# Two tiles per transpose and four half-height silus in a layered sequence kernel on one NeuronCore

## The reference

```python
def body(h, p):
    y = jax.nn.silu(layernorm(h, l1w, l1b))
    y = sconv(y, pr + 1j * pi, lr + 1j * li)     # y[t] = sum over s<=t of p**(t-s) * x[s], real part
    h = h + y * scl
    y = layernorm(h, l2w, l2b)
    y = jax.nn.silu(jnp.einsum('bld,fd->blf', y, w1) + b1_)
    y = jnp.einsum('blf,df->bld', y, w2) + b2_
    return h + y
```

## Time and profile before

| | |
|---|---|
| median of 3 runs | 204.45 us (204.21 to 204.62) |
| the profiled execution, its own time | 204.57 us |
| span of its trace | 202.8 us |
| PE busy | 181.9 us, 90% |
| DVE busy | 157.4 us, 78% |
| ACT busy | 109.8 us, 54% |
| POOL busy | 84.0 us, 41% |
| granted TensorE clock, mean | 0.992 |

### The profile page before, as it was taken

How to read it: one execution, slowest core, us unless ns; L and a number is a source line. 1 busy time by engine, 2 the same in 40 slices (tenths; PEclk the granted TensorE clock), 3 DMA queues, 4 the chain that set the end, 5 groups by cost and what they waited for, 6 DMA issues and landing times.

```text
span 202.8 us, 3759 instructions
## 1 busy us (share of the span) xinstructions
PE 181.9 (90%) x1210; PEld 148.8 (73%) x1210; DVE 157.4 (78%) x547; ACT 109.8 (54%) x281; POOL 84.0 (41%) x142
## 2 busy tenths in 40 slices
PE   0797996859999998999999899999999898988992
PEld 0797995758988788788998689989988444555430
DVE  6898978886588768784977776655899997998872
ACT  1595687524456467637555445462836585863210
POOL 4222269724044422343224522467462735555400
PEclk9999999978999999999999999999999999999999
DMA  5999990000000000000000000000000000002675
GB/s 158 419 376 400 417 368 14 5 0 0 0 5 0 0 3 0 0 3 0 0 0 5 0 0 0 3 0 3 2 0 2 0 3 0 2 0 105 228 283 216
DMA packets 5505, 15.31 MB, mean 75 GB/s; under 512 B 925, under 2 KB 1965, under 8 KB 4462
## 3 DMA queue, kind: packets, MB, share of 16 engines
q1 hardware_dynamic: 5486, 15.07, 19.7%
HBM read 10.87 MB, written 4.19 MB: 74 GB/s over the span
## 4 chain that ended last, share of the span: by engine, by line
PE 68%; DVE 7%; POOL 7%; DMA 6%; ACT 5%; issue 3%; SPq 2%; DVEq 0%; ACTq 0%
PE bank L1508 15%; PE bank L1400 11%; PE bank L1632 7%; PE bank L1490 6%; DMA M<-in_mraw 6%; PE bank L1464 4%; PE bank L1452 4%; POOL RS L360 4%; PE bank L1567 3%; PE bank L1638 3%; POOL M L380 2%; PE bank L1440 2%; PE bank L1556 2%; ACT XA L593 2%; DVE Z L1001 1%
## 5 line engine op out<-in xcount | busy, mean ns | idle before, releaser
L360 POOL TENSOR_TENSOR RS<-SS,nhalf 128x4 f32<-128x4 f32 x36 | 42.9, 1202 | 67.9 <-DVE SS L995 67.6
L1508 PE MATMUL bank<-ffst,HD 128*128 128x128 f32 x256 | 32.7, 283 | 0.0
L1508 PEld LDWEIGHTS bank<-ffst,HD 128*128 128x128 f32 x256 | 31.3, 200 | 0.2
L995 DVE TENSOR_REDUCE SS<-SQ 128x4 f32<-128x260 f32 x36 | 15.2, 421 | 20.9 <-ACT SQ L635 20.3
L1400 PE MATMUL bank<-M,XT 128*128 128x226 f32 x128 | 27.6, 362 | 0.1
L659 ACT ACTIVATE HD<-bank,b1r 128x512 f32<-128x512 f32 x32 | 20.3, 684 | 10.9 <-PE bank L1490 10.8
L1400 PEld LDWEIGHTS bank<-M,XT 128*128 128x128 f32 x128 | 23.2, 189 | 3.6 <-issue 3.1
L635 ACT ACTIVATE SQ<-bank 128x256 f32<-128x256 f32 x36 | 13.8, 383 | 19.6 <-PE bank L1508 9.6
L640 ACT ACTIVATE Y<-bank,cvst 128x512 f32<-128x512 f32 x16 | 12.5, 779 | 15.1 <-PE bank L1452 15.1
L1035 DVE TENSOR_TENSOR_SCAN V<-cvst,U 128x514 f32<-128x514 f32 x16 | 19.5, 1218 | 0.0
L1490 PE MATMUL bank<-Z,w1r 64*128 64x256 f32 x128 | 18.1, 402 | 0.4
(11 more groups left out here) (265 smaller groups left out, 346.0 us busy)
## 6 DMA issues: line engine op xcount, KB each, us to landing
XT<-in_xT SPq DMA_DIRECT2D x4, 1024.0 KB, 11.7
X<-in_x SPq DMA_DIRECT2D x4, 1024.0 KB, 14.0
out<-X SPq DMA_DIRECT2D x8, 512.0 KB, 2.9
w1r<-in_w1d SPq DMA_DIRECT2D x1, 516.0 KB, 16.5
lt<-in_late SPq DMA_DIRECT2D x1, 449.5 KB, 16.3
M<-in_mraw SPq DMA_DIRECT2D x1, 448.0 KB
w2r<-in_w2n SPq DMA_DIRECT2D x1, 256.0 KB, 11.8
winr<-in_win SPq DMA_DIRECT2D x1, 254.0 KB, 2.6
```

Source lines behind the costliest of these rows:

```text
L360: pool.tensor_tensor(RS[:, g, :], SS[:, g, :], nhalf[:, :], ALU.pow).then_inc(done, 1)
L995: dve.tensor_reduce(SS[:, g, :], SQ[:, g, :, :], AX.X, ALU.add).then_inc(done, 1)
L1508: last = pe.matmul(HK[g][:, j * P:(j + 1) * P], HD[:, u % 2, a, at:at + P], ffst[:, L, a * P:(a + 1) * P], start=False, stop=True, skip_gr ...
```

## The change

Units 0 to 3 keep the old transposes and silu. From unit 4 the first half of a unit works in another layout:

- DVE writes the scaled state once (`scale`, 128 x 256) in place of twice (`scale_twice`, 128 x 512). This holds for units 4 to 15, since the first four are written out in `first_steps`.
- `turn1` does two transposes, each of a 128 x 128 block that holds two tiles: the features of tiles 0 and 2 of the group come out on partitions 0 to 63, those of tiles 1 and 3 on partitions 64 to 127, in columns 0 to 255 of bank 0.
- `silu1` is four instructions of 64 partitions x 256 columns: each half of the partitions is read twice and written to the real half and to the imaginary half of `Y`.
- In `setup_late(1)` the product `aux_values @ Wvd.T` is no longer formed by four matmuls; the stored `vpT` is transposed.

```diff
             def silu1(u):
                 g, L = u % GROUPS, u // GROUPS
                 act.wait_ge(t1, u + 1)
-                act.activation(by_seq(Y[:, g, :])[:, :, 1:SL], by_seq(T1B[:, :]), ACT.Silu,
-                               bias=cvst[:, L, LB0:LB0 + 1], scale=cvst[:, L, LW0:LW0 + 1]).then_inc(y1, 1)
+                if u < GROUPS:
+                    act.activation(by_seq(Y[:, g, :])[:, :, 1:SL], by_seq(T1B[:, :]), ACT.Silu,
+                                   bias=cvst[:, L, LB0:LB0 + 1], scale=cvst[:, L, LW0:LW0 + 1]).then_inc(y1, 1)
+                    return
+                for lo in (0, DIM):
+                    for to in (0, DIM):
+                        at = 1 + lo // DIM * P
+                        last = act.activation(by_seq(Y[to:to + DIM, g, :])[:, :, at:at + P],
+                                              by_seq(T1B[lo:lo + DIM, 0:HW]), ACT.Silu,
+                                              bias=cvst[lo:lo + DIM, L, LB0:LB0 + 1],
+                                              scale=cvst[lo:lo + DIM, L, LW0:LW0 + 1])
+                last.then_inc(y1, 1)
...
                 if s < UNITS:
-                    scale_twice(s)
+                    scale(s, rs1, z1)
...
                 if i == 1:
-                    for c in range(VC):
-                        pe.matmul(LB[:, 0:VB], vals[:, c, :], wvd[:, c, :], start=(c == 0), stop=(c == VC - 1))
+                    pe.transpose(LB[:, 0:VB], vpT[:, :], ident[0:VB, 0:VB])
...
-                for j in range(GT):
+                for j in range(2 if GROUPS <= u < UNITS else GT):
```

## The result

The changed kernel takes 214.25 us in the median (213.47 to 215.68, 4 runs) beside 204.33 for the kernel before (4 runs): a ratio of 1.0485 with an interval of 1.045 to 1.052. It is 9.9 us slower where I forecast 1.4 us faster, and lies far outside the range. The profiled execution took 213.60 us, 9.03 more than that of before. Some executions of some kernels here took a few per cent longer than the others of the same kernel; the times are medians of all executions, the ratios compare the others alone.

A forecast was written before the change was run, and what follows sets the result against it. PE, busy 90% and holding 68% of the chain, was taken as the bound, with room on ACT; step terms summed to -1.43 us, giving 203.14 from the profiled 204.57, stated as 203.1 us, eight-in-ten range 201.3 to 205.8.

The forecast's parts named there:

- plain steps: Steps such as 11 to 13: forecast 6.11 us for 6.23; 6.23 or more would show the prediction wrong.
- I take p = 0.465 us per silu: ACT, start to start of half-height silus: 561 ns less 0.10 overlap; four hold ACT 1.86 us where one held 0.68.
- My own slope, 42 us per us of p: ACT from first silu to `z_out`: the change moves by 40 to 42 us per us of time per silu.
- Rival A: ACT, first silu to `z_out`: silus do not overlap, 0.56 us each, sum +2.6, about 207.1 us; chance 0.16.
- `mix_in` and `project` are due earlier than ACT's list reaches them: PE operations between silu and `hidden`: claimed due early enough that their waits have cover; no cost counted.
- the formula 2.75 + 0.25n: ACT's list from silu start to `hidden` after the change, 0.25 us per x copy, against PE's 2.90 us.
- the transposes at 0.11 us each: PE, `turn1`: two fewer transposes give 0.22 us in each of 12 units, 2.6 us if all on the path.
- the state at 0.29: DVE: scaled state falls from 691 to 401 ns, 0.29 us per unit, counting only where PE waits for it.
- the arithmetic of steps 5 to 9: `hidden` to `hidden`, steps 5 to 9: -0.22, -0.74, -0.15, +0.30 and -0.01 us, from PE's and ACT's lists.
- step 8 as a loss: Step 8, where copies keep the silu 3.29 us after `hidden`: 6.32 for 6.02 us, +0.30.
- step 14 at 6.85: Step 14, where the state comes late behind `score_rows`: -0.51 us, from shorter state and transposes.
- the memory product: PE, step 6: a transpose of about 0.11 us replaces 1.08 us, some 0.9 us of PE gone, once.

The follow-up runs named there:

- e12: Changed kernel, all four silus reading and writing only partitions 0 to 63, upper half of Y left out: 207.76 us, ratio 1.018.
- e11: Changed kernel, silus only on partitions 0 to 63 (upper half of Y left out) and x copies in front of silu1: 202.57 us, ratio 0.990.
- e5: Changed kernel with the x copies of a step moved on ACT from behind silu1 to in front of it: 209.60 us, ratio 1.021.
- e9: Changed kernel with silu1 as two silus of 128 partitions x 256 columns, half of Y holding wrong tiles' features: 201.68 us, ratio 0.987.
- e4: Kernel before with silu1 from unit 4 as two full-height silus of 128 partitions x 256 columns: 204.54 us, ratio 1.000.
- e10: Changed kernel with weight and bias of the four silus left out: 205.51 us, ratio 1.005.
- e6: Kernel before with the memory product as a transpose of vpT and score_rows split into steps 14 and 15: 202.70 us, ratio 0.989.

## Why the prediction was wrong

By its own steps, in us from `hidden` to `hidden`. Steps 5 to 9 have no x copies, the others have (from the timelines of PE; steps 12 and 13 are as step 11 within 0.01):

| step | before | predicted | e12 | e11 | changed |
|---|---|---|---|---|---|
| 4 | 7.77 | 7.90 | 8.42 | 7.60 | 8.94 |
| 5 | 6.00 | 5.78 | 5.79 | 5.78 | 6.21 |
| 6 | 6.04 | 5.30 | 5.26 | 5.27 | 5.80 |
| 7 | 6.76 | 6.61 | 6.54 | 6.54 | 7.17 |
| 8 | 6.02 | 6.32 | 6.25 | 6.24 | 6.89 |
| 9 | 5.95 | 5.94 | 5.85 | 5.86 | 6.50 |
| 10 | 7.92 | 8.17 | 8.42 | 7.86 | 8.95 |
| 11 | 6.23 | 6.11 | 6.66 | 6.02 | 7.15 |
| 14 | 7.36 | 6.85 | 7.51 | 6.87 | 8.01 |
| 15 | 6.24 | 6.11 | 6.65 | 6.02 | 7.15 |

I had said that I was wrong if plain steps took 6.23 us or more; they took 7.15 to 7.16. Two steps of the argument failed, and between them they make up the miss: for 4 to 15 the forecast is 70.99 - 1.56 = 69.43 us. e12, which has the overlap back, takes 72.24, so the overlooked wait makes 2.81; the changed kernel takes 78.15, so the lost overlap makes 5.91 more. Step 4 adds 0.52 and 0.52.

**"I take p = 0.465 us per silu."** This is the larger one. The duration of 561 ns was right (560 measured); the 0.10 of overlap was not. p is 0.575. The rows from which I took the overlap were of pairs in which both instructions start at partition 0. In the stretch 4 to 15 this costs 5.9 us (changed against e12). My own slope, 42 us per us of p, makes 4.6 of it. Of the other 1.3, about 0.6 is that the overlapping silus of e12 are 0.45 apart and not 0.465, and about 0.6 that `z_out` follows `square` 0.13 later in steps 5 to 9 (both are estimates from the rows above; in the steps with copies `z_out` waits for `turn2` anyway). Rival A was this mechanism, with p = 0.56, and with a chance of only 0.16. Its argument against itself, that an operation with both operands had overlapped, did not bear on what was new: the change of halves.

**"`mix_in` and `project` are due earlier than ACT's list reaches them", and the formula 2.75 + 0.25n.** It has `turn2` free. `turn2` writes into PSUM bank 1, where the results of `project_x` stand until the copies L575 have read them, so its code has `pe.wait_ge(xa_read, tiles)`; and these copies stand behind the silus on ACT. In the kernel before they were done 0.4 to 0.7 us before `turn2` was due (in step 12 at 104.93), so its row has no wait:

```profile
105.59 0.38 PE L1477 MATMUL bank<-ident,Z 128*128 128x128 f32 x2
```

Against the forecast this wait costs 2.8 us in the stretch (e12). Moving the copies away gives more, 3.8 us (e12 against e11) to 4.1 us (changed against e5), and 0.8 to 1.0 in step 4, since it also takes them out of the list. I read waits from the trace and from ACT's list, and did not list what else the operations behind the silu release. That is also the main reason why rival A's 207.1 us was too low.

What held, in the kernels in which ACT has room: the transposes at 0.11 us each (e9's plain steps are 0.21 to 0.22 us shorter), the state at 0.29 (step 14), the arithmetic of steps 5 to 9 within 0.09 us of e12, step 8 as a loss even at the forecast p, step 14 at 6.85 (e9 and e11 6.87), the memory product (the 5.22 that PE alone would need in step 6 stands in the prediction without its working; e9 took 5.26). DVE's busy time fell by 3.7 us (3.5 forecast); ACT's rose by 17.6 in place of 12 to 14, which is the lost overlap. PE's fell by 1.8 in place of 3.5; in e9, with the same PE work and fewer waits, it fell by 3.6 (178.3), so the work went as forecast.

The Trainium skill (ScalarE: Activation LUTs, What ACT_TABLE_LOAD costs) lets back-to-back ACTIVATEs overlap by about 93 ns. e4 and e12 agree (0.10), the changed kernel and e10 do not (none). The 93 ns per pointer operand that the Trainium skill gives in the same section agree: 560 less 378 ns is 182 for two.

Open stays what in ACT ties the overlap to the first partition, and whether the pointers alone make the 0.13 us between `square` and `z_out`.

## What to carry over

An engine that is busy half of the time can still be the next bound: count its list from the instruction that grows to each instruction behind it that releases another engine, by the semaphores in the code, since a wait that is met in time does not show in a trace. On ACT, the four pieces on changing halves cost four full durations here (2.31 us to the next start); four pieces that kept their first partition cost 1.81. And a reordering that puts small copies in front of the long operation can be worth more than the work that was saved: 4.1 us (changed against e5) beside 3.8 (e9). It did not save this change: e5 is still slower than the kernel before, and of the kernels that compute the whole result only e6, which leaves the silu as it was, is faster by more than its interval.

## What was not expected of the hardware

Two ACT instructions in a row that start at the same partition were 0.10 us closer than their duration (0.46 for 0.56). If the first partition of the output alone, or of the input and the pointers alone, differed, the distance was the duration plus some 0.015 us, with pointers (0.575 for 0.560) and without (0.39 for 0.378). The same first partition was not always enough: `square` and `z_out` were 0.40 to 0.41 apart, no overlap (`square` lasts 0.38), where the silus before them had had their pointers on the upper half. The height of the operation did not matter: 64 and 128 partitions of 256 columns took 0.560 and 0.565 us.
